# Fewer pauses of GpSimd between gathers, carries by VectorE's transposes, and merged loads in a graph network kernel

## What is computed

```python
xl = (x @ Wl + bl).reshape(n, heads, outc)
e_feat = jax.nn.leaky_relu(xl[src] + (x @ Wr + br).reshape(n, heads, outc)[dst], NEG_SLOPE)
logits = jnp.einsum('ehc,hc->eh', e_feat, att)
m = jax.ops.segment_max(logits, dst, num_segments=n)
a = jnp.exp(logits - m[dst])
denom = jax.ops.segment_sum(a, dst, num_segments=n)
a = a / denom[dst]
out = jax.ops.segment_sum(xl[src] * a[:, :, None], dst, num_segments=n)
```

## Time and profile before

| | us |
|---|---|
| median of 3 runs | 8285.53 |
| lowest, highest | 8282.69, 8302.3 |
| profiled execution, its own time | 8275.22 |
| its span | 8273.2 |
| mean granted clock of TensorE | 0.696 of 2.4 GHz |

### The profile page before, as it was taken

One profiled execution on the slowest core, in us unless ns is written; L12 is line 12 of the kernel. 1 busy time (PEld: TensorE's weight loads), 2 busy tenths in 40 slices (PEclk: granted clock), 3 DMA queues, 4 the chain that ended last, 5 costly groups with the idle time before them and its releaser, 6 DMA issues.

```text
span 8273.2 us, 114570 instructions
## 1 busy us (share of the span) xinstructions
PE 5435.2 (66%) x30380; PEld 4591.5 (55%) x30380; DVE 4759.2 (58%) x13239; ACT 4443.8 (54%) x10857; POOL 4817.3 (58%) x4843
## 2 busy tenths in 40 slices
PE   5777777777777765666656665666566666566656
PEld 3666666666666455555555554535555555455544
DVE  3555565555565555656556655655556556565556
ACT  3555555555555454555555655545555556555546
POOL 2666666666666166666666666626666666666640
PEclk8777777777777666666666666656666666666666
DMA  4333333333332322222222222242222222222221
GB/s 115 86 84 84 85 85 84 78 90 77 84 92 76 89 53 53 53 52 51 53 53 53 54 53 52 49 88 53 52 54 54 53 54 53 53 50 53 53 49 47
DMA packets 469478, 538.50 MB, mean 65 GB/s; under 512 B 196815, under 2 KB 377749, under 8 KB 461495
## 3 DMA queue, kind: packets, MB, share of 16 engines
q0 software_dynamic: 154752, 327.15, 17.7%
q1 hardware_dynamic: 314679, 210.82, 9.7%
HBM read 485.07 MB, written 52.43 MB: 65 GB/s over the span
## 4 chain that ended last, share of the span: by engine, by line
another core or an unknown queue 20%; POOL 18%; issue 18%; DVE 15%; PE 14%; ACT 9%; DMA 5%; DVEq 0%; POOLq 0%; ACTq 0%; SPq 0%
POOL xl_g L633 18%; DMA xl_g<-xl_tab,idx 4%; PE PS L694 3%; PE PS L727 3%; ACT dist L854 3%; DVE z L1133 3%; DVE am L1140 2%; PE PS L666 2%; DVE msg L1226 2%; ACT distT L879 2%; PE PS L720 2%; DVE relu_logit L1149 1%; PE PS L683 1%; DVE relu_logit L1152 1%
## 5 line engine op out<-in xcount | busy, mean ns | idle before, releaser
L633 POOL DMA_INDIRECT xl_g<-xl_tab,idx x4836 | 4816.5, 996 | 3179.9 <-issue 2328.3
L727 PE MATMUL PS<-msg,S 128*128 128x137 f32 x9672 | 1699.2, 338 | 895.9 <-DVE msg L1226 588.1
L879 ACT ACTIVATE distT<-PS,neg_p 128x512 f32<-128x512 f32 x1302 | 847.1, 651 | 2521.4 <-remote 1821.0
L727 PEld LDWEIGHTS PS<-msg,S 128*128 128x128 f32 x9672 | 1530.5, 236 | 1022.8 <-issue 943.8
L694 PE MATMUL PS<-xr_w,ST 128*128 128x132 f32 x9672 | 2032.1, 373 | 86.0 <-DVE z L1133 44.4
L1133 DVE TENSOR_TENSOR z<-PS,xl_g 128x528 f32<-128x528 f32 x1302 | 863.6, 663 | 1977.4 <-remote 1251.5
L694 PEld LDWEIGHTS PS<-xr_w,ST 128*128 128x128 f32 x9672 | 1820.8, 275 | 153.6 <-issue 128.6
L854 ACT ACTIVATE dist<-node_row,neg_dst 128x128 f32<-128x128 f32 x4836 | 1534.5, 386 | 0.0
L683 PE MATMUL PS<-rel,sel 26*128 26x128 bf16 x4836 | 640.9, 267 | 1058.2 <-ACT distT L879 593.9
L683 PEld LDWEIGHTS PS<-rel,sel 26*128 26x128 bf16 x4836 | 348.5, 111 | 1348.4 <-ACT distT L879 675.5
L1140 DVE SCALAR_TENSOR_TENSOR am<-z,att_relu 128x512 f32<-128x512 f32 x1302 | 852.6, 655 | 6.5
(11 more groups left out here) (198 smaller groups left out, 4005.1 us busy)
## 6 DMA issues: line engine op xcount, KB each, us to landing
xl_g<-xl_tab,idx POOLq DMA_INDIRECT x4836
ea<-edge_attr SPq DMA_DIRECT2D x62, 1248.0 KB
xr_w<-xr_tab SPq DMA_DIRECT2D x186, 66.0 KB
dst_r<-dst SPq DMA_DIRECT2D x744, 13.0 KB
node_row<-node_id SPq DMA_DIRECT2D x186, 64.0 KB
xl_tab<-xl_g SPq DMA_DIRECT2D x30, 330.0 KB, 3.7
xr_tab<-xl_g SPq DMA_DIRECT2D x30, 330.0 KB, 5.0
st_old<-state SPq DMA_DIRECT2D x124, 68.0 KB
```

What stands on the lines that cost most here:

```text
L633: pool.indirect_dma_start(xl_g[:, q, t, :], None, xl_tab[:, :], bass.IndirectOffsetOnAxis(idx[:, q, t:t + 1], 0))\
L727: last = pe.matmul(agg_ps, S[:, q, t, :], msg[:, t, :], start=t == 0, stop=t == TILES - 1)
L879: act.activation(distT[:, (q + g) % 2, 0:n], spread_ps[:, 0:n], ACT.Abs, bias=neg_p[:, 0:1]).then_inc(spread_read, 1)
```

## The change

- **Pauses.** The landing of gathers is now counted over ten sets (`SETS`: tiles 0-3, 4-6, 7, 8-11, 12-14, 15, 16-19, 20-22, 23, 24-25). GpSimd waits for landings only ahead of tiles 8, 16 and 24, there for all gathers of the item up to the last but one (`PAUSE_FOR`: sets 0-1, 2-4, 5-7). `msg_done` is waited for at every fourth tile as before. VectorE waits ahead of `z` for the sets that hold its group.
- **Carries.** Rows of edges are now 32 per head (26 used), so 128. VectorE's 32 x 32 transposes bring the ends of the runs side by side per head and the carries back; L704, L705, L708, L709 and L1206 are gone. The scans take 26 numbers in each of 128 rows.
- **Spread.** Each target number is split once, at the start, into two digits (number / 128 and the rest) in bf16, kept in the DRAM table `digit_tab`. One matmul with two rows per group rebuilds the number on all partitions; the window's first node goes into ScalarE's bias (`neg_node`). `rel` and `sel` are gone.
- **Loads.** `idx`, `dst_e` and `dst_next` are one array, `dst_r` comes once with 128 rows in place of four times with 26, `tile_ends` is made from `dst_r` by a copy and a transpose, and the digits come in. Ten DMAs per item become five.
- The space reserved for descriptors of indirect DMAs in SBUF is 8192 bytes per partition, which had its default before.

The diff at its core:

```diff
+PACE = 8
+PAUSES = range(PACE, TILES, PACE)
+STEPS = sorted({PACE * b - 1 for b in range(1, len(PAUSES) + 1)} | {g[-1] + 1 for g in GROUPS})
+SETS = [range(a, b) for a, b in zip([0] + STEPS[:-1], STEPS)]
+SET_OF = [m for m, tiles in enumerate(SETS) for t in tiles]
+PAUSE_FOR = {t: [m for m, tiles in enumerate(SETS) if max(t - PACE - 1, 0) <= tiles[-1] < t - 1] for t in PAUSES}
...
-ITEM_DMAS = 5 + HEADS
+ITEM_DMAS = 4
...
+            sp.wait_ge(digits_made, 4)
+            for w in range(2):
+                sp.dma_start(digit_tab[w].rearrange("c (h e) -> (c h) e", h=2), all_digits[w]).then_inc(digits_out, 16)
+            sp.wait_ge(digits_out, 32)
...
-                def edges(a):
-                    return a[bass.ds(ch, 1), :, :].rearrange("a p t -> (a p) t")
-
-                sp.dma_start(idx[:, q, :], edges(src_t)).then_inc(idx_loaded[q], 16)
-                sp.dma_start(dst_e[:, q, :], edges(dst_t)).then_inc(item_loaded[q], 16)
-                sp.dma_start(dst_next[:, q, :], edges(next_t)).then_inc(item_loaded[q], 16)
-                rows = dst[bass.ds(ch, 1), :, :]
-                for h in range(HEADS):
-                    sp.dma_start(dst_r[h * TILES:(h + 1) * TILES, q, :], rows.rearrange("a t e -> (a t) e")).then_inc(item_loaded[q], 16)
-                with nc.allow_non_contiguous_dma(reason="first and last of each tile"):
-                    sp.dma_start(tile_ends[:, q, :, :], rows[:, :, 0:P:P - 1]).then_inc(item_loaded[q], 16)
+                sp.dma_start(edges[:, q, :, :].rearrange("p w t -> p (w t)"), edges_t[bass.ds(ch, 1), :, :].rearrange("a p n -> (a p) n")).then_inc(idx_loaded[q], 16)
+                sp.dma_start(dst_r[:, q, :], dst_rows[bass.ds(ch, 1), :, :].rearrange("a r e -> (a r) e")).then_inc(item_loaded[q], 16)
+                sp.dma_start(digits[:, q, :], digit_tab[:, bass.ds(ch, 1), :].rearrange("w a e -> w (a e)")).then_inc(item_loaded[q], 16)
...
-                        for g, tiles in enumerate(GROUPS):
-                            pool.wait_ge(msg_done[g], pairs * (2 * stage) + 2 * i + (q + 1))
-                            pool.sem_inc(spacer, 1)
-                            if g:
-                                pool.wait_ge(most_gathered[g - 1], (pairs * (2 * stage) + 2 * i + (q + 1)) * (16 * (len(GROUPS[g - 1]) - 1)))
+                        v = pairs * (2 * stage) + 2 * i + (q + 1)
+                        for t in range(TILES):
+                            for m in PAUSE_FOR.get(t, ()):
+                                pool.wait_ge(gathered[m], v * (16 * len(SETS[m])))
                                 pool.sem_inc(spacer, 1)
-                            for t in tiles:
-                                pool.indirect_dma_start(xl_g[:, q, t, :], None, xl_tab[:, :],
-                                                        bass.IndirectOffsetOnAxis(idx[:, q, t:t + 1], 0))\
-                                    .then_inc(gathered[q][g] if g == NG - 1 or t == tiles[-1] else most_gathered[g], 16)
+                            if t % 4 == 0:
+                                pool.wait_ge(msg_done[t // 4], v)
+                                pool.sem_inc(spacer, 1)
+                            pool.indirect_dma_start(xl_g[:, q, t, :], None, xl_tab[:, :],
+                                                    bass.IndirectOffsetOnAxis(idx[:, q, t:t + 1], 0))\
+                                .then_inc(last_gathered[q] if SET_OF[t] == len(SETS) - 1 else gathered[SET_OF[t]], 16)
...
-                        for n, t in enumerate(GROUPS[g]):
-                            last = pe.matmul(spread_ps[:, n * P:(n + 1) * P], sel[:, t, :], rel[:, q, :], start=True, stop=True)
-                        last.then_inc(spread, 1)
+                        a, n = GROUPS[g][0] * P, len(GROUPS[g]) * P
+                        pe.matmul(spread_ps[:, 0:n], digit_w[:, :], digits[:, q, a:a + n], start=True, stop=True).then_inc(spread, 1)
...
-                        act.activation(distT[:, (q + g) % 2, 0:n], spread_ps[:, 0:n], ACT.Abs, bias=neg_p[:, 0:1]).then_inc(spread_read, 1)
+                        act.activation(distT[:, (q + g) % 2, 0:n], spread_ps[:, 0:n], ACT.Abs, bias=neg_node[:, q:q + 1]).then_inc(spread_read, 1)
...
+            dve.wait_ge(dst_in, 16)
+            dve.tensor_scalar(all_digit, all_dst, DIGIT.bit_length() - 1, None, ALU.arith_shift_right).then_inc(digits_made, 1)
+            dve.tensor_scalar(all_dst, all_dst, DIGIT - 1, None, ALU.bitwise_and).then_inc(digits_made, 1)
+            dve.wait_ge(digits_made, 2)
+            dve.tensor_copy(all_digits[0], all_digit).then_inc(digits_made, 1)
+            dve.tensor_copy(all_digits[1], all_dst).then_inc(digits_made, 1)
...
-                    dve.tensor_scalar(rel[:, q, :], dst_r[0:TILES, q, :], node_row[0:TILES, q, 0:1], None, ALU.subtract)
+                    dve.sem_inc(spacer, 1)
+                    dve.wait_ge(idx_loaded[q], use * 16)
+                    dve.tensor_tensor(out=neg_node[:, q:q + 1], in0=neg_p[:, :], in1=node_row[:, q, 0:1], op=ALU.subtract)
...
-                    dve.tensor_tensor(out=tile_eq[:, 1:TILES], in0=first[:, 1:TILES], in1=last[:, 0:TILES - 1], op=ALU.is_equal)
-                    dve.tensor_tensor(out=tile_one[:, :], in0=first, in1=last, op=ALU.is_equal).then_inc(flag_done[2], 1)
+                    dve.tensor_copy(ends[:, :, :], dst_r[:, q, 0:P:P - 1].unsqueeze(2).to_broadcast([P, 2, SQ])).then_inc(flag_done[2], 1)
+                    dve.wait_ge(flag_done[2], v * 3 - 2)
+                    dve.transpose(ends_T[:, :, :].rearrange("p a t -> p (a t)"), ends[:, :, :].rearrange("p a t -> p (a t)")).then_inc(flag_done[2], 1)
+                    dve.wait_ge(flag_done[2], v * 3 - 1)
+                    dve.tensor_tensor(out=tile_eq[:, 1:TILES], in0=ends_T[:, 0, 1:TILES], in1=ends_T[:, 1, 0:TILES - 1], op=ALU.is_equal)
+                    dve.tensor_tensor(out=tile_one[:, :], in0=ends_T[:, 0, 0:TILES], in1=ends_T[:, 1, 0:TILES], op=ALU.is_equal).then_inc(flag_done[2], 1)
...
+                    dve.wait_ge(runs_done, v)
+                    dve.transpose(run_T[:, 0, :], run_up[:, P - SQ:P])
+                    dve.transpose(run_T[:, 1, :], run_down[:, 0:SQ]).then_inc(open_done, 1)
                     dve.wait_ge(open_done, v)
-                    dve.tensor_tensor_scan(open_max[:, 0, 1:LH + 1], through_pen[:, 0, :], open_ps[0], -BIG, ALU.add, ALU.max)
-                    dve.tensor_tensor_scan(open_max[:, 1, 1:LH + 1][:, ::-1], through_pen[:, 1, :][:, ::-1], open_ps[1][:, ::-1], -BIG,
+                    dve.tensor_tensor_scan(open_max[:, 0, 1:TILES + 1], through_pen[:, 0, :], run_T[:, 0, 0:TILES], -BIG, ALU.add, ALU.max)
+                    dve.tensor_tensor_scan(open_max[:, 1, 1:TILES + 1][:, ::-1], through_pen[:, 1, :][:, ::-1], run_T[:, 1, 0:TILES][:, ::-1], -BIG,
                                            ALU.add, ALU.max).then_inc(openmax_done, 1)
                     dve.wait_ge(openmax_done, v)
-                    dve.tensor_tensor(out=carry[:, 0, :], in0=open_max[:, 0, 0:LH], in1=enter_pen[:, 0, :], op=ALU.add)
-                    dve.tensor_tensor(out=carry[:, 1, :], in0=open_max[:, 1, 2:LH + 2], in1=enter_pen[:, 1, :], op=ALU.add).then_inc(carry_done, 1)
+                    dve.tensor_tensor(out=carry[:, 0, 0:TILES], in0=open_max[:, 0, 0:TILES], in1=enter_pen[:, 0, :], op=ALU.add)
+                    dve.tensor_tensor(out=carry[:, 1, 0:TILES], in0=open_max[:, 1, 2:TILES + 2], in1=enter_pen[:, 1, :], op=ALU.add).then_inc(carry_done, 1)
+                    dve.wait_ge(carry_done, v)
+                    dve.transpose(carry_T[:, :, :].rearrange("p a t -> p (a t)"), carry[:, :, :].rearrange("p a t -> p (a t)")).then_inc(carryT_done, 1)
 
                 def maxima():
 
                     q, v, use = closes
                     dve.wait_ge(carryT_done, v)
-                    dve.tensor_copy(carry_col[:, :], carry_ps).then_inc(carrycol_done, 1)
-                    dve.wait_ge(carrycol_done, v)
-                    dve.tensor_tensor_scan(up[:, :], row_pen[:, 0:P], lt_ps, carry_col[:, 0:1], ALU.add, ALU.max).then_inc(up_done, 1)
+                    dve.tensor_tensor_scan(up[:, :], row_pen[:, 0:P], lt_ps, carry_T[:, 0, SQ - 1:SQ], ALU.add, ALU.max).then_inc(up_done, 1)
                     dve.wait_ge(up_done, v)
-                    dve.tensor_tensor_scan(seg_max[:, ::-1], row_pen[:, 1:P + 1][:, ::-1], up[:, ::-1], carry_col[:, 1:2], ALU.add, ALU.max)\
+                    dve.tensor_tensor_scan(seg_max[:, ::-1], row_pen[:, 1:P + 1][:, ::-1], up[:, ::-1], carry_T[:, 1, 0:1], ALU.add, ALU.max)\
...
-    nc = bacc.Bacc("TRN2", target_bir_lowering=False, num_devices=1)
+    nc = bacc.Bacc("TRN2", target_bir_lowering=False, num_devices=1, dynamic_dma_scratch_size=8192)
```

121 lines of the change are left out of this document (62 added, 59 removed).

## The result

The changed kernel takes **9484.6 us** (median of 4 runs, 9423.8 to 9520.9) where the kernel before, timed beside it, takes 8293.9 (4 runs, 8282.7 to 8314.4): a ratio of **1.142, 95% interval 1.137 to 1.148**. Slower by 14%, where 5% faster was forecast.

The account below looks back on a forecast made before the run. Two paths of almost equal rate, GpSimd's gathers and the other engines, were taken to bound it. GpSimd's 565 us less 135 coming back, set-up +6: 8275 - 430 + 6 = 7851 us; own range 7700 to 7990, full 7655 to 8135.

Parts of the forecast that it names:

- What bounds the kernel: Item loop: GpSimd's gathers with pauses and the other engines' path have almost equal rate; no engine's work alone sets the end.
- Pauses: GpSimd's gather loop: three of six pauses an item go, 558 x 1.01 = 565 us off GpSimd; bounds 0 and 565.
- Carries: VectorE's scans without TensorE's products: about 2 us per item, 370 us, on the second path; bounds 150 and 803.
- Spread, flags, penalties, loads: One spread matmul for four, VectorE's copy and transpose, three ScalarE penalties for four, five DMAs for ten: 0 gain.
- Set-up: Splitting target numbers on VectorE at the start and two stores before the node rows: +6 us, bounds 0 and 20.
- The sum: Whole kernel: 565 us less 135 coming back as waits gives 430; 8275 - 430 + 6 = 7851 us; chance 0.52.
- (a): The second path binds, gaining only `carry_col`'s 149 us: 8132 us; sign, message waits beyond 500 us; chance 0.21.
- (b): TensorE's clock rises without its stand at L708, GpSimd alone binds: 7634 us; sign, clock above 0.75; chance 0.12.
- (c): TensorE's clock falls as it loses small products, a fall of 0.04 costing 700 us: 8551 us; chance 0.05.
- (d): VectorE's new copy and four transposes hold GpSimd up 1.0 us an item, 186 us: 8037 us; chance 0.06.
- the rule beside it: Trainium skill: a VectorE copy, cast or tensor_scalar can take the port pair shared with GpSimd and block it; gives 8037.
- (e): Each remaining GpSimd pause is longer by as much as two were, so nothing is left: 8280 us; chance 0.04.

Follow-up runs that it names:

- late job: Any job of runs on one chip that is not prompt, TensorE's semaphores changing late after their records; the kernel before took 8072 to 8298 us in five.
- prompt one: A job where nine in ten of TensorE's semaphores change within 0.01 us of the records, in every kernel traced; kernel before 8145 and 8041 us.
- few gathers: Changed kernel with 10 of 26 gathers an item in stages 2 and 3, output not the reference's: 6393.5 us, again 6364.0 us, semaphores not late both times.
- small additions: Changed kernel plus GpSimd's wait for z of group 5 (7682.6 us), 30 TensorE products an item in stages 2 and 3 (7679.0), or 24 unused-semaphore increments ahead of three gathers (7634.4).
- filler kernel: Changed kernel plus 30 bf16 products of 256 columns an item on TensorE in stages 2 and 3: 7679.0 us (0.943), with late semaphores 9429.3 us (1.168).
- gaps that wait for no landing: Changed kernel plus 24 increments of an unused semaphore on GpSimd ahead of gathers 4, 12 and 20: 8599.4 us (1.034) with late semaphores, 7634.4 (0.949) otherwise.

## Why the prediction was wrong

- **What bounds the kernel.** Right that two paths share the loop and that an edit on one is worth its sum only if the other keeps up. Wrong on what the earlier trace rows showed: the 1251.5 us of remote waits were taken for ordinary waits for products, and the item of 40.4 us in the earlier trace rows for one of a low clock. They go with late semaphores: the mean delay is 2.5 us in that item and 0.1 in the next, of 27.2 us.
- **Pauses, the step that failed.** The step of the prediction reads "565 us off GpSimd", with bounds "0 if all comes back as waits for messages, 565": nothing below zero, as if a pause cost only GpSimd its time. GpSimd did lose it (2438.8 for 2450 us). But in a late job removing three pauses of six cost 12.3% in the kernel before (9085.3 for 8091.0), and putting them back brought the changed kernel, at 1.131 to 1.145 of before in its own jobs, to 1.010. With three pauses the second path, not GpSimd, has the longer items, 45 us, held up by waits for TensorE's late semaphores (2814.9 us remote before `z`).
- **Carries.** The durations were near: transposes 0.17 to 0.25 us for 0.2, the scans of 26 columns 0.21 and 0.19 for 0.2, the additions 0.19 and 0.18 for 0.17, and no wait stands before them. Their 370 us can't be seen in a late job. In a prompt one the second path needs 26.0 us an item in stages 2 and 3 (few gathers), far below GpSimd's 36, so there they are worth nothing that these runs show.
- **Spread, flags, penalties, loads.** 0, as forecast: undoing the spread gave nothing back.
- **Set-up.** +6, bounds 0 to 20: the stages begin 17 us later.
- **The sum.** In prompt jobs, three kernels that are the changed one with small additions ran at 0.943, 0.943 and 0.949 of before; the forecast was 7851/8275 = 0.949, with 37.9 us an item where they need 36.4 or less. They are 462, 466 and 407 us faster, for 424 forecast. That GpSimd gains is borne out there; the size is in part luck, since the 135 us that the sum let come back as waits for messages do not appear in those traces, and the 565 us are not reached either. The changed kernel itself met late semaphores in all four jobs it was in, and that it would take about 7680 us in a prompt one is inferred from those three, not measured.
- **Rivals.** (a) had the sign of its mark, messages waited for beyond 500 us (2020.7), and its mechanism, the second path binding, but priced it at a gain. (b) did not come. (c) had the side and its mark, under 0.65 in stages 2 and 3 (0.64), but not the cause: in the filler kernel the clock is higher and the items longer. Its price, 13.2 us for 0.14 of clock, was read from the two items above, which differ in delay too. In the example the granted clock is 1.00 from 4022 to 4030 us, while `expanded` is already late, and 0.50 from 4033 to 4037, after TensorE stood for 5.46 us; so here the fall follows the wait. The Trainium skill, TensorE: Matmul & The Clock Gate, HAM oscillation, which the prediction used for (b), does not account for the loss: with the fillers the clock rose and the time did too. (d) did not come: gathers average 979 ns, 996 before, beside the new copies and transposes. Its 8037 was not what the rule beside it gives either: the prediction quotes that for a copy, cast or tensor_scalar, and four of the five instructions priced are transposes. (e) did not: pauses are 1.2 us, not 2.

**What holds the semaphores is not settled.** Shown: they change late in five jobs of seven (that of the result among them), in every kernel traced there; the pauses decide what that costs; neither clock, nor amount of work, nor GpSimd's lead accounts for it. Argued only: that a run of gathers holds them. For it speak the table of delays and the gaps that wait for no landing. In the fourteen traces of late jobs some 10,100 changes within the items have two gathers or fewer in the 8 us before them, and not one is late by over 1 us. Against a simple form of it speaks that one semaphore of the example (4038.17) changed in the middle of a run of gathers. The few gathers were never seen in a late job, which would have decided it. Open too is the recording itself: in late jobs 4 to 30% of TensorE's semaphore changes, 27 to 39% of VectorE's and 18 to 39% of ScalarE's are missing from the trace, in prompt ones under 1%. The Trainium skill, NOTIFIC — the notification-queue block, Overflow: three behaviours, one of which stalls the engine, says that a full queue of records can drop them or hold the engine that writes them. The missing records agree with the first. Semaphores held and then let go in a row would fit the second, but no run here shows it, or what the times would be unrecorded: that rival is untested.
